# Sums of squares on a second column tile of TensorE, and a DMA that brings their row back to partition 0

## What is computed

```
xn   = (x - mean(x)) / sqrt(var(x) + 1e-5)          # over the 1024 features
attn = softmax(causal(q k^T / 32)) v                # q, k, v = xn Wq^T, xn Wk^T, xn Wv^T
w4   = clip(round(kernel / s), -8, 7) * s           # s = max|kernel| / 7
out  = x + attn + xn w4 + bias + (xn a) b           # x: (4, 4096, 1024) f32
```

## Time and profile before

| | us |
|---|---|
| median of 3 runs | 978.63 (978.46 to 979.85) |
| the profiled execution, whole | 979.23 |
| its span, first to last instruction, slowest core (core 7) | 977.7 |
| spans of the 8 cores | 969.2 to 977.7 |
| median span, die 0 and die 1 | 974.3, 973.2 |
| phase 1, to the barrier | about 0 to 403 |
| phase 2 | about 403 to 601 |
| phase 3 | the rest |

### The profile page before, as it was taken

One profiled execution on the slowest core, in us unless ns is written; L12 is line 12 of the kernel. 1 busy time (PEld: TensorE's weight loads), 2 busy tenths in 40 slices (PEclk: granted clock), 3 DMA queues, 4 the chain that ended last, 5 costly groups with the idle time before them and its releaser, 6 DMA issues.

```text
span 977.7 us, 12171 instructions; the slowest of 8 cores (969.2 to 977.7 us)
## 1 busy us (share of the span) xinstructions
PE 745.6 (76%) x3191; PEld 316.1 (32%) x3191; DVE 471.8 (48%) x782; ACT 272.7 (28%) x617; POOL 41.0 (4%) x70
## 2 busy tenths in 40 slices
PE   0046899989989899348889793769979979788872
PEld 0011333433334344113334341324434434343330
DVE  1245386676865868433734511457135161524443
ACT  0013333334333333133231010030442334333431
POOL 2000000000000000100000000000000101010111
PEclk9997899989999999759989897779999989998986
DMA  8970104314133111490252225875225235121334
GB/s 176 218 128 1 43 1 108 65 44 107 21 89 65 44 65 44 67 168 9 92 125 87 85 86 189 266 234 181 89 98 194 109 111 190 45 109 43 130 131 171
DMA packets 35316, 103.32 MB, mean 106 GB/s; under 512 B 2706, under 2 KB 15252, under 8 KB 30772
## 3 DMA queue, kind: packets, MB, share of 16 engines
q0 software_dynamic: 22720, 44.11, 20.5%
q1 hardware_dynamic: 12532, 58.43, 16.6%
HBM read 92.11 MB, written 29.36 MB: 124 GB/s over the span
## 4 chain that ended last, share of the span: by engine, by line
PE 61%; DVE 14%; issue 10%; DMA 8%; ACT 5%; DVEq 0%; SPq 0%; ACTq 0%; POOL 0%; POOLq 0%
PE psAV L915 15%; PE psS L815 12%; PE psK L366 10%; PE psV L393 6%; PE psQ L599 5%; PE psF L630 4%; DMA w<-wker 4%; DMA qtile<-qT_h 2%; PE psT L900 2%; PE T L298 1%; DMA xga<-xcols 1%; PE T L294 1%; DVE ab_sb L251 1%; PE T L325 1%; DVE xg L346 1%
## 5 line engine op out<-in xcount | busy, mean ns | idle before, releaser
L915 PE MATMUL psAV<-v_res,ptb 128*128 128x512 bf16 x544 | 151.9, 385 | 20.5 <-ACT ptb L906 11.7
L393 PE MATMUL psV<-wvb,xg 128*128 128x512 bf16 x512 | 116.1, 387 | 13.0 <-ACT v_res L403 13.0
L906 ACT COPY ptb<-psT 128x128 bf16<-128x128 bf16 x272 | 70.6, 266 | 171.0 <-PE psT L900 168.7
L366 PE MATMUL psK<-xg,wkb 128*128 128x512 bf16 x512 | 114.0, 383 | 4.5 <-ACT kst L372 2.9
L815 PE MATMUL psS<-k_res,qtile 128*128 128x512 bf16 (+1 forms) x240 | 65.8, 440 | 49.4 <-DMA qtile<-qT_h 29.8
L915 PEld LDWEIGHTS psAV<-v_res,ptb 128*128 128x128 bf16 x544 | 51.9, 97 | 91.4 <-issue 68.1
L934 DVE SCALAR_TENSOR_TENSOR outsb<-psAV,invl,fft 128x512 f32<-128x512 f32 x16 | 12.0, 750 | 133.2 <-PE psT L900 72.3
L393 PEld LDWEIGHTS psV<-wvb,xg 128*128 128x128 bf16 x512 | 50.3, 99 | 77.7 <-issue 22.5
L366 PEld LDWEIGHTS psK<-xg,wkb 128*128 128x128 bf16 x512 | 50.3, 99 | 66.8 <-issue 8.3
L827 DVE CAST scores<-psS 128x512 bf16<-128x512 f32 x72 | 47.5, 660 | 50.2 <-PE psS L815 49.6
L815 PE MATMUL psS<-kbuf,qtile 128*128 128x512 bf16 (+1 forms) x336 | 68.4, 364 | 0.0
(11 more groups left out here) (101 smaller groups left out, 750.4 us busy)
## 6 DMA issues: line engine op xcount, KB each, us to landing
kbuf<-kT_h SPq DMA_DIRECT2D x21, 1024.0 KB, 6.5
w<-wker SPq DMA_DIRECT2D x16, 512.0 KB, 6.6
xg<-xfm POOLq DMA_DIRECT2D x8, 1024.0 KB, 10.9
kT_h<-kst SPq DMA_DIRECT2D x8, 1024.0 KB, 3.8
ff_h<-ffst SPq DMA_DIRECT2D x16, 512.0 KB, 2.8
fft<-ff_h POOLq DMA_DIRECT2D x16, 512.0 KB, 6.3
xrt<-xrows POOLq DMA_DIRECT2D x16, 512.0 KB, 6.9
out<-outsb POOLq DMA_DIRECT2D x16, 512.0 KB, 3.0
```

The costliest lines, as they stand in the source:

```text
L366: P.op("T", lambda e, g=g, dc=dc, cc=cc: e.matmul(psK[dc % 2][:, :], wkb[:, :].rearrange("p (a x) -> p a x", a=NCH)[:, cc, dc * 128:(dc + ...
L393: P.op("T", lambda e, g=g, tt=tt, h=h, cc=cc: e.matmul(psV[tt % 2][h][:, :], xg[g % 3][:, cc * G1 + tt * 128: cc * G1 + (tt + 1) * 128], w ...
L906: ptb_ev[kc] = P.op("S", lambda e, kc=kc: e.copy(out=ptb[kc % 3][:, :], in_=psT_[kc % 2][:, :]), waits=wv, inc=chS)
L915: av_lastk[kc] = P.op("T", lambda e, si=si, kc=kc, h=h, nk=nk: e.matmul(psAV[si % 2][h][:, :], ptb[kc % 3][:, :], v_res[:, kc * C + h * 51 ...
```

## The change

The sums of squares go to row 32 of T1 instead of row 0, and both stats matmuls are given a tile position: (0, 0) for the sums, (0, 32) for the sums of squares. Rows on different partitions can't be combined by VectorE, so the sums of squares are copied to partition 32 of a new tile `strow32` and a DMA, issued by GpSimd, moves them to partition 0. The 1/sqrt row is written over the same row (`tr2 = s2r`). Phase 2 is changed in the same way.

```diff
-    strow = sb1("strow", [1, 4 * G1], F32)
+    strow = sb1("strow", [1, 3 * G1], F32)
+    strow32 = sb1("strow32", [33, G1], F32)
...
-    s1r, s2r, tr1, tr2 = (strow[0:1, i * G1:(i + 1) * G1] for i in range(4))
+    s1r, s2r, tr1 = (strow[0:1, i * G1:(i + 1) * G1] for i in range(3))
+    tr2 = s2r
...
             P.op("T", lambda e, g=g, cc=cc: e.matmul(
                 T0[0:1, :], onescol[:, 0:1], xg[g % 3][:, cc * G1:(cc + 1) * G1],
-                start=(cc == 0), stop=(cc == NCH - 1), skip_group_check=True),
+                start=(cc == 0), stop=(cc == NCH - 1), skip_group_check=True,
+                tile_position=(0, 0)),
                 waits=w, inc=chT)
             sq_T[(g, cc)] = P.op("T", lambda e, g=g, cc=cc: e.matmul(
-                T1[0:1, :], onescol[:, 0:1], sqb[cc % 2][:, :],
-                start=(cc == 0), stop=(cc == NCH - 1), skip_group_check=True),
+                T1[32:33, :], onescol[:, 0:1], sqb[cc % 2][:, :],
+                start=(cc == 0), stop=(cc == NCH - 1), skip_group_check=True,
+                tile_position=(0, 32)),
                 waits=[sq_S[(g, cc)]], inc=chT)
...
-        v1 = P.op("V", lambda e, s2=s2: e.tensor_copy(out=s2, in_=T1[0:1, :]), inc=chV)
+        v32 = P.op("V", lambda e: e.tensor_copy(out=strow32[32:33, :], in_=T1[32:33, :]),
+                   waits=[g_s2mv.get(g - 1)], inc=chV)
+        v1 = P.op("G", lambda e, s2=s2: e.dma_start(out=s2, in_=strow32[32:33, :]),
+                  waits=[v32], inc=chG)
+        g_s2mv[g] = v1
```

More of the change, by code:

```diff
@@ L264, in build_nc @@
     psV = [[ps1(f"psV{i}_{h}", [128, 512]) for h in range(2)] for i in range(2)]
-    s1r, s2r, tr1, tr2 = (strow[0:1, i * G1:(i + 1) * G1] for i in range(4))
+    s1r, s2r, tr1 = (strow[0:1, i * G1:(i + 1) * G1] for i in range(3))
+    tr2 = s2r
     xg_dma, stats_T, math_V, bcast_T, bcastev_V, xn_V = {}, {}, {}, {}, {}, {}
-    math_S, xn_cc = {}, {}
+    math_S, xn_cc, g_s2mv, g_s2mv2 = {}, {}, {}, {}
     vmm_T, kst_Y, kst_S, vmm_S = {}, {}, {}, {}
@@ L486, in build_nc @@
     sqa = [sb2(f"sqa{i}", [128, G1], BF16) for i in range(2)]
-    strow2 = sb2("strow2", [1, 4 * G1], F32)
+    strow2 = sb2("strow2", [1, 3 * G1], F32)
+    strow32b = sb2("strow32b", [33, G1], F32)
     mbc2 = sb2("mbc2", [128, G1], F32)
@@ L498, in build_nc @@
     psF = [[ps2(f"psF{i}_{h}", [128, 512]) for h in range(2)] for i in range(2)]
-    s1a, s2a, ta1, ta2 = (strow2[0:1, i * G1:(i + 1) * G1] for i in range(4))
+    s1a, s2a, ta1 = (strow2[0:1, i * G1:(i + 1) * G1] for i in range(3))
+    ta2 = s2a
     wq_dma = None
@@ L529, in e_stats2 @@
                 U0[0:1, :], onescol[:, 0:1], xga[b % 3][:, cc * G1:(cc + 1) * G1],
-                start=(cc == 0), stop=(cc == NCH - 1), skip_group_check=True),
+                start=(cc == 0), stop=(cc == NCH - 1), skip_group_check=True,
+                tile_position=(0, 0)),
                 waits=w, inc=chT)
             sq2_T[(b, cc)] = P.op("T", lambda e, b=b, cc=cc: e.matmul(
-                U1[0:1, :], onescol[:, 0:1], sqa[cc % 2][:, :],
-                start=(cc == 0), stop=(cc == NCH - 1), skip_group_check=True),
+                U1[32:33, :], onescol[:, 0:1], sqa[cc % 2][:, :],
+                start=(cc == 0), stop=(cc == NCH - 1), skip_group_check=True,
+                tile_position=(0, 32)),
                 waits=[sq2_S[(b, cc)]], inc=chT)
@@ L540, in e_math2 @@
                   waits=[stats2_T[b]] + list(prev), inc=chV)
-        v1 = P.op("V", lambda e: e.tensor_copy(out=s2a, in_=U1[0:1, :]), inc=chV)
+        v32 = P.op("V", lambda e: e.tensor_copy(out=strow32b[32:33, :], in_=U1[32:33, :]),
+                   waits=[g_s2mv2.get(b - 1)], inc=chV)
+        v1 = P.op("G", lambda e: e.dma_start(out=s2a, in_=strow32b[32:33, :]),
+                  waits=[v32], inc=chG)
+        g_s2mv2[b] = v1
         v2 = P.op("V", lambda e: e.tensor_tensor(
```

## The result

| | before | changed |
|---|---|---|
| median of the runs, us | 978.6 | 1019.6 |
| ratio, undisturbed runs, with its 95% interval | | 1.0413 (1.0401 to 1.0424) |
| the profiled execution, us | 979.23 | 1018.4 |
| its span, slowest core | 977.7 | 1016.9 |
| mean granted clock, core by core | 0.907 to 0.913 | 0.875 to 0.886 |

The change makes the kernel 4.1% slower.

What follows compares the result with a forecast made beforehand. TensorE was taken to wait for the end of math, not of the stats. −1.0 + 25.3 + 8.9 + 0 + 13.2 = 46.4 on the profiled 979.23 gave 1025.6, as a median 1025.0 us; range 1003 to 1045.

Steps and rivals of the forecast that it cites:

- stats, first group of a phase: Phase 1's first group: paired stats matmuls side by side save 1.0 us (0 to 1.4); phase 2's gain is swallowed.
- eleven moves: In eleven groups the DMA of the squares' row lengthens math by 2.3 us each, all path; +25.3 (17.6 to 37.4).
- first move of phase 2: Group 0 of phase 2: the row's DMA stands behind wqb's load on GpSimd's queue; +8.9 us, 11.3 at most.
- the clock: TensorE runs at the low clock after longer waits, new in six of eight places, 2.2 us each; +13.2 (3.3 to 21.6).
- What bounds the kernel: In all 12 groups TensorE waits for the end of math, not of the stats; 13.0 us in six V waits.
- The weights: The term for wqb's load holding up the first move of phase 2; +8.9 us.
- The moved loads: Loads of x and xga now issued behind moves cost 0, up to 2 us if HBM is slower then.
- Slow stats on a parted array: Rival: each of 16 stats matmuls takes 0.4 us more, math starts 3.0 later in up to 12 groups; +36, 1061; 7%.
- Faster, because the stats are path: Rival: shorter stats save 12 × 1.2 = 14 us if the move were hidden, giving 964 us; 3%.

Runs made afterwards that it cites:

- the move alone: Changed kernel with both stats matmuls back on row 0, the squares' row still sent through the DMA; 1019.0 us, ratio 1.0385.
- the tiles alone: Changed kernel without the DMA: VectorE copies the squares' row straight from PSUM partition 32 to SBUF partition 0; 985.3 us, ratio 1.0043.
- the issue order: Changed kernel with the load of wqb issued behind the first move of phase 2 instead of ahead of it; 1011.5 us, ratio 1.0324.
- The filled waits: Changed kernel with 18 extra matmuls, results never read, between V's halves in the six groups where TensorE waits; 1007.2 us, ratio 1.027.

## Why the prediction was right, and by how much its terms were off

1025.0 was predicted (1003 to 1045), 1019.6 measured. The mechanism was right in its parts; here are its terms, from the two timelines of the slowest core:

| term | predicted | measured | how it was read |
|---|---|---|---|
| stats, first group of a phase | −1.0 | −0.8 | first stats matmul to L306/L310: 6.41, now 5.63 |
| eleven moves | +25.3 | +19.7 | L306 to L311 1.98; L310 to L319 3.70 to 3.82 in eleven groups |
| first move of phase 2 | +8.9 | +8.7 | L539 to L544 1.98; L551 to L560 10.64 |
| the clock | +13.2 | +10.7 | V's second halves +10.1, the feed-forward +1.7 and −1.1 |
| the rest | 0 | +0.9 | start of phase 1 +2.6, from the last feed-forward matmul on −1.0, remainder −0.7 |
| sum | +46.4 | +39.2 | span 977.7, now 1016.9 |

*What bounds the kernel.* That TensorE waits for the end of math and not for the end of the stats is shown from both sides: the move alone costs 38 of 41 us, the tiles alone gain nothing, and where Ln stands later the wait of 13.0 us is gone. The forecast of 27 to 34 us for the six V waits was missed, they are 24.9: the move is shorter, and one wait is only 2.39, behind a first half that ran at the low clock.

*The eleven moves.* The step that was off is the latency: 2.4 was taken from issue to use, and it was 1.74 (179.28 to 181.02); waking GpSimd took 0.66, where 0.62 had been read from the earlier trace rows. The row that came nearest was SyncE's load of 32 KB in the earlier trace rows with 1.7, not the output with 3.0. What makes the difference stays open: the smallest load of those rows, 0.2 KB and issued by GpSimd as the move is, took 3.5. The Trainium skill, "DMA: Bandwidth & Descriptors" (section "Anatomy of one DMA"), has about 2.0 us fixed; the 1.6 to landing is somewhat below.

*The weights.* Shown by the issue order (8.1 us back). That the move's data stand behind the weights' fits both kernels that issue it on GpSimd's queue: the row is in use 0.4 after wqb lands in the changed kernel, and 0.3 after (460.9, 461.20) with the move alone. On SyncE's queue it was in use 4.4 before wqb landed, and yet took 6.7. So the queue explains the last 2 us and the match with wqb's landing; why the move takes some 5 us longer than alone on the other queue too is not shown. Both have the same cure.

*The clock.* The filled waits give 12.4 us back, where the second halves of V account for 10.1; the remainder is not attributed. Eight low stretches were expected behind the waits; they came in five V groups and one of two feed-forward groups, at 1.7 to 2.9 each. One V group had its low stretch before the wait, where it is free. That the term comes near is part luck: fewer stretches than forecast, some of them dearer. What I hadn't weighed is that the same effect turns the tiles alone into a loss.

*The moved loads.* Their zero held: no V or K group waits for `xg` or `xga` longer than before, and K(0)'s wait of 4.75 is the 2.90 of before plus the move.

*The start of phase 1.* +2.6 on this core, while the other seven cores reached their first stats matmul 0.3 to 2.1 earlier than before. I take it for scatter; no run separates it from the load of x for group 1, which the change moved away from the start.

*The rivals.* Slow stats on a parted array: they aren't, 0.12 between the matmuls of a pair. "Faster, because the stats are path": false for this kernel, and true in part once Ln and the squares' buffers are out of the way. That the price which I had put on it (14 us) is near the 10.9 measured there is luck: the stats save 24.9 there, and over half of it is lost again.

## What to carry to other kernels

Before an engine's work is shortened, look at what its next idle stretch waits for: if that chain doesn't contain the work, the gain becomes idle time, and the idle time may cost clock as well. Here a DMA of 2 KB cost about 2.4 us from the end of the producer to the start of the consumer, and about four times that (9.3) when it was issued behind a load of 2 MB. A copy by VectorE from PSUM partition 32 to SBUF partition 0 took the 0.68 us of the copy that stood there anyway, so the DMA was not needed at all. The order of small operations on an in-order engine (here Ln ahead of a PSUM copy, with VectorE's empty instruction gone as well) was worth 29 us, and only after it and two more buffers was the tile trick worth its 11.

## What the runs showed of the hardware that I had not expected

- A small DMA on SyncE's queue took 6.7 us to its use while GpSimd's queue carried 2 MB, and 1.7 on GpSimd's queue when nothing was in flight.
- Idle waits of 2.5 to 3.0 us were followed by the low clock in six of six V groups, waits of 1.7 to 2.4 in two of six. But K(0) kept the full clock behind a wait of 3.02, and a feed-forward half behind 3.26. Extra matmuls without a purpose made the kernel 12.4 us faster.
- Two column tiles doubled the rate of the stats matmuls at a granted clock of 0.50 (1.2 GHz): pairs started 0.43 us apart, where single matmuls did. With the step to V it was 1.7 times (6.4 us against 3.7). The Trainium skill, "TensorE: Matmul & The Clock Gate" (Part 3, on packing small matmuls), has 2.38 for three column tiles; no run here has three, and the two agree in kind.
